# An LSTM layer on one core: row scales for Wx, float32 recurrent parts of steps 1 and 2, and weight loads begun by two queues

## What is computed

```python
xW = jnp.einsum('ntd,dg->ntg', x, Wx) + b
def step(carry, xw_t):
    prev_h, prev_c = carry
    a = xw_t + prev_h @ Wh
    i, f, o = (jax.nn.sigmoid(a[:, k * Hd:(k + 1) * Hd]) for k in range(3))
    g = jnp.tanh(a[:, 3 * Hd:])
    next_c = f * prev_c + i * g
    next_h = o * jnp.tanh(next_c)
    return ((next_h, next_c), next_h)
return x + jnp.swapaxes(hs, 0, 1)
```

## Time and profile before

| | us |
|---|---|
| median of three runs | 2572.32 |
| the profiled execution, whole | 2571.03 |
| its span, first to last instruction | 2569.2 |
| TensorE busy | 2519.4 |
| VectorE busy | 2125.0 |
| ScalarE busy | 1535.5 |
| GpSimd busy | 51.3 |

### The profile page before, as it was taken

The page is one execution under the profiler, slowest core; times in us unless marked ns, Lnnn a source line. Parts: engine busy times, 40 slices in busy tenths (PEclk is TensorE's granted clock), DMA queues, the critical chain, the costliest instruction groups (busy, mean ns, idle before and its releaser), DMA issues.

```text
span 2569.2 us, 166266 instructions
## 1 busy us (share of the span) xinstructions
PE 2519.4 (98%) x67392; PEld 1803.4 (70%) x67392; DVE 2125.0 (83%) x8738; ACT 1535.5 (60%) x5780; POOL 51.3 (2%) x134
## 2 busy tenths in 40 slices
PE   4999999999999999999999999999999999999998
PEld 1677777777777777777777777777777777777775
DVE  7888888888888888888888888888888888888887
ACT  5666565566656556565656656566665655666564
POOL 0000000000000000000000000000000000000000
PEclk7999999999999999999999999999999999999999
DMA  6111111111111111111111111111111111111111
GB/s 157 39 41 37 42 44 37 37 47 39 37 43 43 37 37 46 39 37 43 43 37 38 47 37 37 44 42 37 39 47 37 37 45 41 37 40 46 37 37 27
DMA packets 223581, 109.84 MB, mean 43 GB/s; under 512 B 25280, under 2 KB 222528, under 8 KB 222528
## 3 DMA queue, kind: packets, MB, share of 16 engines
q1 hardware_dynamic: 223456, 109.45, 17.0%
q10 hardware_dynamic: 96, 0.03, 0.0%
HBM read 75.83 MB, written 33.55 MB: 43 GB/s over the span
## 4 chain that ended last, share of the span: by engine, by line
PE 96%; DVE 1%; SPq 1%; DMA 1%; ACT 1%; issue 0%; ACTq 0%; DVEq 0%
PE Z L345 71%; PE run L345 19%; PE extra L345 6%; DMA wh_raw<-in_Wh 1%; SPq L262 1%; DVE wx_lo L766 0%; ACT wx_hi L552 0%; SPq L293 0%; ACT tanh_c L534 0%; DVE h_hi L834 0%; DVE wh_lo L771 0%; ACT wh_lo L562 0%; ACT wh_hi L556 0%; SPq L301 0%; ACT act L523 0%
## 5 line engine op out<-in xcount | busy, mean ns | idle before, releaser
L345 PE MATMUL Z<-wh_hi,hT_hi 128*32 128x512 f16 x8176 | 796.1, 379 | 9.6 <-DVE hT_hi L839 6.2
L345 PE MATMUL Z<-wh_lo,hT_hi 128*32 128x512 f16 x8176 | 796.1, 379 | 0.0
L523 ACT ACTIVATE act<-Z 128x128 f32<-128x128 f32 x1024 | 287.6, 281 | 591.7 <-PE Z L345 591.7
L345 PE MATMUL Z<-wh_hi,hT_lo 128*32 128x512 f16 x8176 | 529.7, 379 | 0.0
L534 ACT ACTIVATE tanh_c<-gc 128x64 f32<-128x64 f32 x1024 | 262.8, 257 | 312.6 <-DVE gc L860 248.7
L345 PE MATMUL run<-wx_hi,x_hi 128*32 128x256 f16 x6096 | 431.0, 273 | 14.3 <-DVE x_lo L671 13.8
L345 PE MATMUL Z<-wx_hi,x_hi 128*32 128x256 f16 x6096 | 430.7, 273 | 0.9 <-DVE wx_lo L766 0.5
L345 PE MATMUL run<-wx_lo,x_hi 128*32 128x256 f16 x6096 | 431.0, 273 | 0.0
L345 PE MATMUL run<-wx_hi,x_lo 128*32 128x256 f16 x6096 | 431.0, 273 | 0.0
L345 PE MATMUL Z<-wx_hi,x_lo 128*32 128x256 f16 x6096 | 430.7, 273 | 0.0
L345 PE MATMUL Z<-wx_lo,x_hi 128*32 128x256 f16 x6096 | 430.7, 273 | 0.0
(11 more groups left out here) (91 smaller groups left out, 4024.2 us busy)
## 6 DMA issues: line engine op xcount, KB each, us to landing
x_in<-in_x SPq DMA_DIRECT2D x512, 64.0 KB, 2.1
x_res<-in_x SPq DMA_DIRECT2D x512, 64.0 KB, 2.1
out_y<-y SPq DMA_DIRECT2D x508, 64.0 KB, 1.7
wx_raw<-in_Wx SPq DMA_DIRECT2D x16, 256.0 KB, 8.7
wh_raw<-in_Wh SPq DMA_DIRECT2D x16, 256.0 KB, 16.4
bias_bc<-in_bias SPq DMA_DIRECT2D x4, 64.0 KB, 2.2
out_y<-y SPq DMA_DIRECT2D x4, 48.0 KB, 1.6
h_in<-in_h SPq DMA_DIRECT2D x4, 16.0 KB, 13.0
```

Of the source, the lines that this page charges most:

```text
L345: return nc.tensor.matmul(out, lhsT, rhs, start=False, stop=last, skip_group_check=True)
L523: nc.scalar.activation(half_gates(act, a)[:, 0:2], half_gates(Z[s], a)[:, 0:2], ACT.Sigmoid, scale=scale).then_inc(gates_done, 1)
```

## The change

1. Wx is scaled by row: each partition has its own power of two for each cp, from the sum of magnitudes of its rows in chunks cp and 2+cp. ScalarE takes these sums (`sum_of_wx`) in place of VectorE's `largest_wx`; `scale_of_rows` makes the scale with three small operations on the same partition. x is multiplied by the inverse (`x_scale(r, cp)`), so `scale_x` becomes two instructions of 256 columns. The maximum over the partitions remains for the scale of z alone.
2. The cuts are ordered by cp, and the chunks of Wx are loaded and used in the order 0, 2, 1, 3. T4 is made earlier, and no cut of Wx is left for block 0.
3. The steps 1 and 2 take h @ Wh in float32 from `wh_raw` (`raw_recurrent_part`), with plain gates; `scale_raw` stays for Z[3] alone. The hi/lo split of h begins with step 2.
4. SP issues the partition tiles j = 0, 1 of Wx and Wh, GpSimd the tiles j = 2, 3; ScalarE issues x of block 0 and the bias ahead of its first activation.
5. Block 0 is a list of its own on TensorE, ScalarE and VectorE.

```diff
...
+        RAW = 2
...
+        LOWER = (0, 1)
+        UPPER = (2, 3)
...
-            load_x(0, 0)
-            for j in range(NJ):
-                sp.dma_start(bias_bc[L * j:L * j + B].rearrange("p (g c) -> p g c", g=4),
-                             bias_view[j].partition_broadcast(B)).then_inc(bias_loaded, 16)
-            load_weights(sp, wx_raw, wx_view, wx_loaded, TURNS)
...
+            load_weights(sp, wx_raw, wx_view, wx_lower, WX_ARRIVE, LOWER)
             for j in range(NJ):
                 sp.dma_start(h0_in[L * j:L * j + B], h0_view[j]).then_inc(h0_loaded, 16)
             load_x(1, 1)
-            load_weights(sp, wh_raw, wh_view, wh_loaded, TURNS)
+            load_weights(sp, wh_raw, wh_view, wh_lower, range(NCH), LOWER)
             load_res(0, 0)
...
-            for ch in range(NCH):
-                pe.wait_ge(wx_loaded[ch], 16 * NJ)
+            for ch in WX_ARRIVE:
+                pe.wait_ge(wx_lower[ch], 16 * len(LOWER))
+                pe.wait_ge(wx_upper[ch], 16 * len(UPPER))
...
+            def raw_recurrent_part(t):
+                pe.wait_ge(h_turned, t + 1)
+                for ch in range(NCH):
+                    if t == 0:
+                        pe.wait_ge(wh_lower[ch], 16 * len(LOWER))
+                        pe.wait_ge(wh_upper[ch], 16 * len(UPPER))
+                    raw = by_tile(wh_raw[:, ch])
+                    for j in range(NJ):
+                        mm = add(Z[t][L * j:L * j + B, :], h_T[:, ch, :], raw[:, j], ch == NCH - 1)
+                mm.then_inc(z_done, 1)
+            raw_recurrent_part(0)
...
+            def first_block():
+                raw_recurrent_part(1)
+                raw_recurrent_part(2)
+                first_product(2, 0)
+                second_products(2, 0)
+                third_products(2, 0).then_inc(p5_done, 1)
+                first_product(3, 1)
+                pe.wait_ge(z_scaled, 1)
+                recurrent_part(3, 3)
+                second_products(3, 1)
+                last_product(2, 0).then_inc(slot_done, 1)
...
                 if started(n - 2):
                     sc.wait_ge(x_lo_cut, nth(2 * n - 3))
-                nc.scalar.activation(forms[:, r, 0:8].rearrange("p k s -> p (k s)"),
-                                     x_T[:, :, :, :].rearrange("p ch t b -> p (ch t b)"), ACT.Copy,
-                                     scale=x_scale(r)).then_inc(x_scaled, 1)
+                for cp in range(2):
+                    nc.scalar.activation(forms[:, r, 0:8].rearrange("p (f cp e) s -> p cp f (e s)", f=2, cp=2)[:, cp],
+                                         x_T[:, :, :, :].rearrange("p (f cp) t b -> p cp f (t b)", cp=2)[:, cp], ACT.Copy,
+                                         scale=x_scale(r, cp)).then_inc(x_scaled, 1)
...
+                scale = 1.0 if isinstance(t, int) and t <= RAW else z_unscale
...
+            for j in range(NJ):
+                sc.dma_start(x_in[L * j:L * j + B, 0], x_view[j, :, 0:TB, :]).then_inc(x_loaded[0], 16)
+            for j in range(NJ):
+                sc.dma_start(bias_bc[L * j:L * j + B].rearrange("p (g c) -> p g c", g=4),
+                             bias_view[j].partition_broadcast(B)).then_inc(bias_loaded, 16)
...
+            def sum_of_wx(ch):
+                sc.wait_ge(wx_lower[ch], 16 * len(LOWER))
+                sc.wait_ge(wx_upper[ch], 16 * len(UPPER))
+                nc.scalar.activation(wh_hi[:, ch], wx_raw[:, ch], ACT.Abs, accum_out=wsum[:, 0, ch:ch + 1]).then_inc(wx_summed, 1)
...
-            for ch in range(NCH):
-                cut_wx_hi(ch)
-                if ch == 1:
-                    sum_of_x(1, 1, 1)
-                sum_of_wh(ch)
-            cut_wx_hi(4)
+            sum_of_wx(0)
+            sum_of_wx(2)
+            sc.wait_ge(row_scale_done, 1)
+            cut_wx_hi(0, "B11", "B21", "T1")
+            sum_of_wx(1)
+            cut_wx_hi(0, "T2", "T3")
+            sum_of_wx(3)
+            cut_wx_hi(0, "B22", "T4")
+            sc.wait_ge(row_scale_done, 2)
+            cut_wx_hi(1, "B11", "B21")
+            sum_of_wh(0)
+            sum_of_x(1, 1, 1)
+            cut_wx_hi(1, "T1", "T2")
+            sum_of_wh(1)
+            cut_wx_hi(1, "T3", "B22")
+            sum_of_wh(2)
+            cut_wx_hi(1, "T4")
+            sum_of_wh(3)
+            sc.wait_ge(z_done, 1)
+            gates(0, 0)
+            tanh_of_c(0)
             sc.wait_ge(w_scale_done, 2)
             cut_wh_hi(0)
             scale_x(1, 1)
-            scale_raw(1)
-            cut_wh_hi(1)
-            cut_x_hi(2, 1, 1, 0)
-            set_run(2, 0, 1)
-            set_extra(2, 0, 1)
-            sc.wait_ge(z_done, 1)
-            gates(0, 0)
-            cut_wh_hi(2)
-            tanh_of_c(0)
-            cut_wh_hi(3)
-            scale_raw(2)
-            scale_raw(3)
-            set_z_unscale(0, 0)
-            sum_of_x(2, 0, 2)
-            cut_wx_hi(5)
-            cut_wx_hi(6)
+            def first_block():
+                sc.wait_ge(z_done, 2)
+                gates(1, 1)
+                tanh_of_c(1)
+                cut_wh_hi(1)
+                cut_x_hi(2, 1, 1, 0)
+                set_run(2, 0, 1)
+                set_extra(2, 0, 1)
+                cut_wh_hi(2)
+                sc.wait_ge(z_done, 3)
+                gates(2, 2)
+                set_c11(2, 0)
+                tanh_of_c(2)
+                cut_wh_hi(3)
+                set_c12(2, 0)
+                scale_raw(3)
+                set_z_unscale(0, 0)
+                cut_x_hi(3, 1, 1, 1)
+                set_run(3, 1, 1)
+                set_extra(3, 1, 1)
+                take_p5(2, 0)
+                set_c21(2, 0)
+                set_c11(3, 1)
+                sum_of_x(2, 0, 2)
+                sc.wait_ge(z_done, 4)
+                gates(3, 3)
+                tanh_of_c(3)
+                scale_x(2, 0)
+                sum_of_x(3, 1, 2)
+                cut_x_hi(4, 2, 0, 0)
+                set_c12(3, 1)
+                set_run(4, 0, 0)
+                set_extra(4, 0, 0)
+                set_z_unscale(1, 1)
...
+            def scale_of_rows(cp):
+                v.wait_ge(wx_summed, 2 * cp + 2)
+                nc.vector.scalar_tensor_tensor(row_max[:, cp:cp + 1], wsum[:, 0, cp:cp + 1], 2.0 ** (LOW_FIELD - EXP_ONE),
+                                               wsum[:, 0, 2 + cp:3 + cp], ALU.max, ALU.max).then_inc(row_max_done, 1)
+                v.wait_ge(row_max_done, cp + 1)
+                nc.vector.tensor_scalar(row_field[:, cp:cp + 1], row_max[:, cp:cp + 1].bitcast(I32), 255 << MANT, None,
+                                        ALU.bitwise_and).then_inc(row_field_done, 1)
+                v.wait_ge(row_field_done, cp + 1)
+                nc.vector.tensor_scalar(w_scale[:, cp:cp + 1], row_field[:, cp:cp + 1], -1.0,
+                                        float((2 * EXP_ONE + TOP_W) << MANT), ALU.mult, ALU.add).then_inc(row_scale_done, 1)
...
-                for ch in range(NCH):
-                    largest_wx(ch)
-                    if ch < 2:
-                        make_t1(ch)
-                    if ch == 2:
-                        make_t3(0)
+                make_t1(0)
+                make_t3(0)
+                scale_of_rows(0)
+                make_t2(0)
+                cut_wx_lo(0, "B11", "B21")
+                make_t4(0)
+                make_t1(1)
+                cut_wx_lo(0, "T1", "T2", "T3")
+                make_t3(1)
+                scale_of_rows(1)
                 largest_weight(0)
-                make_t3(1)
+                make_t2(1)
+                cut_wx_lo(0, "B22", "T4")
+                cut_wx_lo(1, "B11", "B21")
+                make_t4(1)
                 v.wait_ge(h0_loaded, 16 * NJ)
-                nc.vector.transpose(h0_T[:, :, :], h0_in[:, :].rearrange("p (ch l) -> p ch l", ch=NCH)).then_inc(h0_turned, 1)
+                nc.vector.transpose(h_T[:, :, :], h0_in[:, :].rearrange("p (ch l) -> p ch l", ch=NCH)).then_inc(h_turned, 1)
                 weight_scale(0)
-                make_t2(0)
-                cut_wx_lo(0)
-                make_t2(1)
                 turn_x(1, 1, 1)
-                cut_wx_lo(1)
-                cut_wx_lo(2)
-                cut_wx_lo(3)
+                cut_wx_lo(1, "T1", "T2", "T3", "B22", "T4")
                 largest_weight(1)
-                make_t4(0)
-                make_t4(1)
+                step(0)
                 weight_scale(1)
                 scale_tables()
                 scale_block(0, 0)
                 scale_block(1, 1)
                 set_h_scale(0, 0)
-                cut_wx_lo(4)
                 cut_wh_lo(0)
-                first_forms(1, 1)
-                last_forms(1, 1)
-                cut_wh_lo(1)
-                cut_x_lo(2, 1, 0)
...
+                if isinstance(t, int) and t < RAW:
                     last_c(t)
-                else:
-                    last_c(t)
-                    cut_wh_lo(2)
-                    high_part_of_h(t, 0)
```

(46 more changed lines are left out.)

187 lines of the change are left out of this document (90 added, 97 removed).

## The result

The changed kernel takes 2578.74 us (median of 12 runs, 2577.61 to 2580.64) against 2572.27 for the kernel before, timed beside it: a ratio of 1.0026, interval 1.0019 to 1.0034. It is slower by 6.5 us. The prediction was 2565.8 us with a range up to 2575.5, so it was wrong, and in sign too. The profiled execution took 2578.22 us with a span of 2576.4, 7.2 us more span than before.

The account below looks back on a forecast made before the run. TensorE was taken as the bound, gapless from step 5, so only the start counted: gates of step 0 14.7 us earlier, the stretch to step 5 8.1 longer, sum -6.6; forecast 2572.3 - 6.5 = 2565.8 us, range 2562.0 to 2575.5.

Parts of the forecast that it names:

- The bound: TensorE has no gap from step 5 to 2550 us, so the time moves as much as step 5's start.
- ScalarE's list: ScalarE's work behind the bias, before the gates of step 0: 33.1 us, plus about 1.5 of waits.
- G: Milestone at the start: the gates of step 0, 59.28 us before, forecast at 44.6, 14.7 earlier.
- When the bias lands: Load of the bias at the start: even split of bytes between queues with an allowance, taken as 10 us.
- the bias comes late: Rival in ScalarE's FIFO: at 16 us total 2569.3, at 22 to 24 us 2575 to 2580; later than 23 us: 0.12.
- the cases: Forecast 0.46; bias between 11.5 and 23 us or low clock 0.42; bias later 0.12; side-by-side loads 0.04.
- Both signs: A gap after step 5, or ScalarE seeing the bias after 15 us, would make the prediction wrong.
- From G to step 5: Stretch from the gates of step 0 to step 5: 40.2 us against 32.07, 8.1 later.
- part 1: TensorE's float32 recurrent part of step 1: four groups at 1.2 GHz, 7.1 us.
- No gap behind step 5: TensorE from step 5 on: instructions left as they are, no gap expected behind it.
- GpSimd's issues: GpSimd issuing weight loads: priced at nothing; at 2 us each, gates of step 0 would come 1 to 3 later.
- The load of the weights: Weight loads at the start: 9.24 MB at 235 GB/s, 39 us, last chunk of Wh landing at 41 us.

Follow-up runs that it names:

- e9: Changed kernel with 2 KB weight rows, residual load of block 1 moved ahead, two block-0 reorderings and warm float16 products: 2557.82 us, ratio 0.9945.
- e6: Changed kernel with each weight DMA cut into four of 64 KB with 2 KB rows: 2565.50 us in one execution.
- e15: Changed kernel with SP and GpSimd holding the weights behind chunk 0 of Wx until the bias has landed: 2573.61 us, ratio 1.0007.
- e3: Changed kernel with SP's residual load of block 1 moved ahead of the load of x of block 5: 2576.44 us, ratio 1.0017.
- e10: Changed kernel with each weight load cut into two DMAs with 4 KB rows: 2571.77 us, ratio 0.9999.
- e13: Changed kernel with Wx loaded in 256 KB DMAs of 2 KB rows, Wh as in the changed kernel: 2574.79 us, ratio 1.0010.
- e14: Changed kernel with each weight load cut by partitions into four 64 KB DMAs of eight 8 KB rows: 2605.07 us, ratio 1.0141.

## Why the prediction was wrong

- **The bound.** Right. The stretch behind step 5 costs the same in before and in e9, 2477.85 us, and the time moved with the beginning.
- **ScalarE's list.** Right. The sum was 33.1 + 1.5 = 34.6 us from the bias to G. Measured where the list binds: 34.5 in the changed kernel, 34.1 to 35.8 in eight others (e6 among them, 9.74 to 45.36) with the bias anywhere from 9.3 to 24.8 us. With the bias at its real place my own sum gives 24.8 + 34.6 = 59.4; it was 59.37.
- **When the bias lands.** This step failed. I took an even split of bytes between queues and put the bias at 10 us; it came at 24.83. That is 14.8 us too early, the whole of the -14.7 that the forecast took for G. What the runs show in its place: the queues took turns packet by packet, 221 of ScalarE beside 201 and 213 of the weights in 10 us, so 0.10 MB passed beside 2.31 MB, and the bias was in only when Wx was through. The rival "the bias comes late" had this mechanism, one for one, and the figure (22 to 24 us), and I gave it 0.12. Its prices don't follow from my own sum: at a bias of 16 us that sum gives -0.6 and not "about 3 earlier", at 22 to 24 us +5.4 to +7.4 and not +3 to +5. (The chances of the cases also add to 1.04.) At a bias of 24.8 the sum is +0.1 for G and +8.1 behind it; measured in the span were +0.1, +4.9 and 2.2 behind step 5, by the two terms below. Both signs that I had named as making the prediction wrong came, a bias after 15 us and a gap after step 5. What I should have weighed is how early the other queues hold all of Wx: eight issues at the 0.46 us of the earlier trace rows are 3.7 us for each, and in the changed kernel SP and GpSimd had handed over 4.19 MB by 5.3 us, against ScalarE's 0.52. The page "DMA: Bandwidth & Descriptors" of the Trainium skill, section "Queues, rings and completion order", says turns go by packets and not by bytes; it stood against my step. This trace agrees, by the packets just given, and over the whole wait 0.52 MB came in beside 4.9, where three even shares give 1.0. Turns hold the bias up only as long as the other queues have packets: with their backlog held back it was in at 10.0 us (e15).
- **From G to step 5.** 40.2 us predicted, 37.0 measured (32.07 before). The order of waits was as forecast: x_lo behind `cut_wh_lo`, `set_c12` behind `cut_wh_hi`, x_lo again, `scale_block(2)`. The size was off mainly at one term, 1.95 of the 3.2 us: part 1 at 1.2 GHz throughout was 7.1 us, and it took 5.15 (from 61.76), as the granted clock rose from 0.50 to 1.00 within it, between 64 and 65 us:

```profile
63.00:64.00 1.00, 1.00 (x8) 0.20 (x4) 0.86 (x6) 1.00 (x1) 0.00 (x0) 0.50 0.00 0
64.00:65.00 1.00, 1.00 (x8) 0.20 (x4) 0.96 (x3) 0.85 (x3) 0.00 (x0) 0.57 0.00 0
65.00:66.00 1.00, 1.00 (x16) 0.36 (x12) 1.00 (x1) 0.21 (x1) 0.00 (x0) 1.00 0.00 0
```

- **No gap behind step 5.** Wrong by 1.87 us. I followed each engine's new list but not SP's, whose `load_res(1)` stands behind waits on entries that the change moved to near the end of block 0. e3 shows it.
- **GpSimd's issues** cost 0.50 us each, not 2; with all of Wh landing in time the price of nothing held.
- **The load of the weights.** 235 GB/s was nearly right up to 25 us (231 to 243); from 25 to 45 it was 203 to 217. "The last chunk at 41" was wrong: GpSimd's last issues of Wh came at 32 us, since they stand behind an all-reduce that waits for the late bias, and its queue was busy until past 45 us. With the bias late it didn't matter: no sum of Wh waited for its chunk.
- **`scale_x`** takes 0.90 us for its two halves, hidden in every block, as forecast.

The bytes that pass ahead of the last of x and the bias are much the same in the changed kernel, in e10 and in e13 (from the mean rate up to the bias, less 0.52 MB: 220 x 24.83 = 5.5 to 4.9 MB, 270 x 17.93 = 4.8 to 4.3, 248 x 21.0 = 5.2 to 4.7). Turns one for one fit this: in all three the packets of Wx in either queue (384 to 1152) are no more than the 1152 of x and the bias, so Wx passes nearly whole, and the rate decides when. Not settled: why the small rows get more than their turn in the first microseconds, why two queues of short rows move more, and, as the DMA engines were busy only half of the time in e14, what small DMAs with long rows would do at a share of 1.0.

## What to carry to other kernels

Before a small load that everything waits for is moved to a queue of its own, count how many packets and bytes the other queues will have been handed by then. Price one row of each of them for every row of the small load, until they run out; where the small load has as many rows as they have, all of theirs pass first. A queue of its own is no priority. Put it first in the queue of the bulk load, or hand the bulk over in pieces small enough that no backlog builds up. When a list of work is reordered, walk through every queue whose waits name one of its entries, loads that stand behind such a wait included.
